# Two-block transformer on one core: the layers' first loads inside the causal projection, and four masked units ahead of each attention loop

## The reference, cut to what matters

```
x = x + causal_attention(layernorm(x)) @ wo + bo        # 16 heads of 16
y = layernorm(x)                                        # then two layers on y:
for l in range(2):
    q, k, v = split(shift_token(y) @ wqkv[l])            # 8 heads of 64
    q, k = rotary_xpos(l2norm(q) * q_scale, l2norm(k) * k_scale)
    y = y + local_attention(q, k, v) @ wo2[l]            # window 128, looks one window back
    y = y + (a * gelu(g)) @ w2[l] + b2[l]                # a, g = split(ln(shift(y)) @ w1[l] + b1[l])
x = x + y
```

## Time and profile before

| | us |
|---|---|
| median of 3 runs (2271.04 to 2278.29) | 2271.34 |
| the profiled execution | 2281.7 |
| its span, first to last instruction | 2280.0 |
| PE busy in it | 1991.5 (87%) |
| DVE, ACT, POOL busy | 1458.2, 1243.6, 798.6 |

### The profile page before, as it was taken

The page is one execution under the profiler, slowest core; times in us unless marked ns, Lnnn a source line. Parts: engine busy times, 40 slices in busy tenths (PEclk is TensorE's granted clock), DMA queues, the critical chain, the costliest instruction groups (busy, mean ns, idle before and its releaser), DMA issues.

```text
span 2280.0 us, 36416 instructions
## 1 busy us (share of the span) xinstructions
PE 1991.5 (87%) x12096; PEld 1254.8 (55%) x12096; DVE 1458.2 (64%) x3958; ACT 1243.6 (55%) x2980; POOL 798.6 (35%) x663
## 2 busy tenths in 40 slices
PE   4565899999989745999999999999899899899998
PEld 2232233333323433677677677677667667667666
DVE  5457788888886334756756755756756756756654
ACT  1110666666666422764764764764664664664663
POOL 2223221221132225614614614614623623623620
PEclk9786899999999877999999999999999999999999
DMA  5645765435631361000000000010300000000000
GB/s 145 148 130 113 132 145 85 69 69 74 121 62 72 107 191 49 40 20 19 1 20 19 1 20 19 2 68 15 103 20 19 20 20 19 20 19 20 20 2 28
DMA packets 124457, 129.00 MB, mean 57 GB/s; under 512 B 50460, under 2 KB 101232, under 8 KB 123248
## 3 DMA queue, kind: packets, MB, share of 16 engines
q1 hardware_dynamic: 123696, 117.75, 22.3%
q0 software_dynamic: 576, 8.91, 1.0%
HBM read 75.51 MB, written 50.86 MB: 55 GB/s over the span
## 4 chain that ended last, share of the span: by engine, by line
PE 37%; DVE 11%; ACT 7%; issue 5%; POOL 2%; DMA 0%; DVEq 0%; SPq 0%; POOLq 0%; ACTq 0%
PE qkv_ps L1340 5%; DVE rot_s L1894 5%; PE s_ps L1444 4%; PE o_ps L1525 3%; PE pt_ps L1525 3%; PE s_ps L1386 3%; PE qkv_ps L1402 3%; PE pt_ps L1457 3%; PE o_ps L1482 3%; DVE p_sb L1903 3%; ACT p_sb L1638 3%; PE pt_ps L1444 2%; PE o_ps L1444 2%; POOL inv_norm L1788 2%; PE s_ps L1402 2%
## 5 line engine op out<-in xcount | busy, mean ns | idle before, releaser
L717 ACT ACTIVATE probs<-st_ps 128x512 f32<-128x512 f32 (+3 forms) x768 | 330.0, 494 | 170.7 <-PE st_ps L625 170.4
L1340 PE MATMUL qkv_ps<-w_qkv,x_parts 128*128 128x512 f32 x1152 | 308.5, 411 | 33.8 <-DVE x_parts L1868 24.6
L1638 ACT ACTIVATE p_sb<-p_sb,negmax 128x256 f32<-128x256 f32 (+1 forms) x512 | 249.2, 489 | 64.3 <-DVE negmax L1903 64.1
L610 PE MATMUL s_ps<-k_stack,q_stack 96*128 96x512 bf16 (+3 forms) x768 | 243.2, 348 | 41.5 <-DVE piece_negmax L762 25.9
L762 DVE CUSTOM_DVE_ANT_0 seen<-s_ps,causal 128x128 f32<-128x128 f32 (+3 forms) x512 | 233.6, 484 | 46.9 <-PE s_ps L610 46.7
L1340 PEld LDWEIGHTS qkv_ps<-w_qkv,x_parts 128*128 128x128 f32 x1152 | 211.9, 194 | 81.5 <-issue 40.0
L625 PE MATMUL st_ps<-q_stack,k_stack 98*128 98x512 bf16 (+3 forms) x768 | 242.3, 336 | 15.7 <-ACT probs L717 10.1
L1903 DVE CUSTOM_DVE_ANT_0 p_sb<-s_ps,band 128x256 f32<-128x256 f32 (+1 forms) x512 | 185.4, 401 | 88.8 <-PE s_ps L1386 85.6
L844 POOL TENSOR_SCALAR_AFFINE_SELECT probs<-probs 128x512 f32<-128x512 f32 x128 | 81.6, 637 | 419.5 <-ACT probs L717 419.5
L1796 POOL TENSOR_TENSOR rot_c<-qn,turn_by 128x512 f32<-128x512 f32 x128 | 178.6, 1415 | 129.6 <-PE turn_ps L1366 103.7
L1654 ACT COPY p_t<-pt_ps 128x512 f32<-128x512 f32 (+1 forms) x256 | 143.2, 559 | 126.0 <-PE pt_ps L1457 124.7
(11 more groups left out here) (146 smaller groups left out, 3504.2 us busy)
## 6 DMA issues: line engine op xcount, KB each, us to landing
qk_scratch<-parts SPq DMA_DIRECT2D x64, 192.0 KB, 2.8
q_stack<-qk_scratch SPq DMA_DIRECT2D x96, 128.0 KB, 6.7
k_stack<-qk_scratch SPq DMA_DIRECT2D x96, 128.0 KB, 7.1
w_ffn<-ffn_weights POOLq DMA_DIRECT2D x4, 2176.0 KB, 11.4
v_scratch<-v_out SPq DMA_DIRECT2D x32, 256.0 KB, 2.5
v_sb<-v_scratch SPq DMA_DIRECT2D x16, 512.0 KB, 10.5
x_in<-xt_scratch SPq DMA_DIRECT2D x16, 512.0 KB, 4.2
ffn_weights<-w_high SPq DMA_DIRECT2D x2, 2176.0 KB, 7.9
```

The costliest lines, as they stand in the source:

```text
L610: pe.matmul(s_ps[i % 3][:, 0:kw], q_stack[0:STK, slot, h, qt * P:(qt + 1) * P], k_stack[0:STK, slot, h, k0:k0 + kw], start=True, stop=True ...
L717: act.activation(probs[:, n % 3, h, q0:CH], st_ps[i % 3][:, q0:CH], ACT.Exp).then_inc(exp_done.sem, 1)
L1340: mm = pe.matmul(qkv_ps[:, part * CH:(part + 1) * CH], x_parts[:, w % XR, xp, k, :], w_qkv[:, wp, k, part * INNER:(part + 1) * INNER], sta ...
L1638: act.activation(p_sb[:, u % 4, h, k0:PW], p_sb[:, u % 4, h, k0:PW], ACT.Exp, scale=-1.0, bias=negmax[:, u % 4, h:h + 1], accum_out=total[ ...
```

## The change

It does three things. First, memory for the projection weights, their raw form, the head scales, the tables and the first x_in is taken before `project_causal`, and `att_in` (now eight tiles) and `x_all` stay allocated to the end; several buffers of `layers` are laid over them. SP loads the first eight tiles of attention output at the end of `causal_attention`, and within `project_causal` it issues the weights at steps 4 and 5, the tables at steps 6 to 9, the scales at steps 10 to 13 and the first sequence at steps 20 and 21; ACT casts the weights and DVE scales the tables during the third sequence, DVE subtracts during the fourth. The transposed half is now stored five tiles behind. `layers` no longer does this for layer 0. Second, `EARLY` is 4: at the end of a feed-forward (and ahead of pass 0) four units are scored and masked, tile 1's turns, the q and k projection of tile 3, and the unit vectors and sines of tile 2 are done there too. Third, in the loop DVE masks two units at once, at even u, ahead of x_parts, sums and unit vectors.

```diff
@@ causal_attention, SP
+            def load_first_outputs():
+                att_tiles, att_in = out_in
+                for c in range(NC):
+                    sp.wait_ge(att_stored[c], 16 * (NG + 1))
+                for t in range(AR):
+                    load_outputs(sp, a, att_tiles, t).then_inc(att_in[t], 16)
...
+            load_first_outputs()
             store(B * NG - 1, 1)
@@ project_causal, SP
+            def load_first(i):
+                half, quarter = HD2 // 2, NT // 4
+                for k in range(KD):
+                    if i == NT // 2 + k:
+                        sp.dma_start(raw_w[:, k, :], a["wqkv"][0, k * P:(k + 1) * P, :]).then_inc(raw_in, 16)
+                for q in range(4):
+                    if i == NT - 2 + q:
...
+                for j, name in ((0, "q_scale"), (2, "k_scale")):
...
+                for k in range(KD):
+                    if i == 2 * NT + NT // 2 + k:
+                        for s in xt_stored:
+                            sp.wait_ge(s, 16 * 2)
+                        sp.dma_start(x_first[:, k, k:k + T], a["xt_scratch"][0, k]).then_inc(x_in, 16)
...
             for i in range(B * NT):
+                load_first(i)
...
-                if i + 4 < B * NT:
-                    load(i + 4)
-                store_xt(i - 3)
+                if i + AR < B * NT:
+                    load(i + AR)
+                store_xt(i - 5)
@@ project_causal, ACT
+                if b == 2 and tile(0) is not None and 0 <= tile(0) < 3 * KD:
+                    high_weights(tile(0))
@@ project_causal, DVE
+                if tile(0) is not None and 0 <= tile(0):
+                    if b == 2:
+                        scale_tables(tile(0))
+                    if b == 3 and tile(0) < 3 * KD:
+                        low_weights(tile(0))
@@ layers
-EARLY = 2
+EARLY = 4
@@ layers, PE, attention
-                    if p < 2 and w + 1 < NT:
+                    if p < 2 and 0 < w < NT - 1:
                         turn(it, w + 1, p)
...
-                    if p >= 1 and w + AHEAD < NT:
+                    if u == 2:
+                        project(it, AHEAD, 2)
+                    if p >= 1 and 0 < w < NT - AHEAD:
                         project(it, w + AHEAD, p - 1)
@@ layers, PE, feed_forward (the same behind scores(0, 0) ahead of pass 0)
                 down(1, 0)
+                if more:
+                    turn(it + 1, 1, 0)
+                    scores(it + 1, 1)
+                    turn(it + 1, 1, 1)
                 down(1, 1)
+                if more:
+                    for part in range(2):
+                        project(it + 1, AHEAD, part)
@@ layers, ACT
+            def first_exponentials(it):
+                for u in range(EARLY):
+                    if u >= 2:
+                        copy_turned(it, 1, u - 2)
+                    exponentials(it, u)
@@ layers, DVE, attention
+                    if EARLY <= u < UNITS and u % 2 == 0:
+                        mask_scores(it, u)
+                        mask_scores(it, u + 1)
                     if p == 2 and w + AHEAD + 1 < NT:
                         low_x(it, w + AHEAD + 1)
                     if p == 3 and w + AHEAD < NT:
                         sums(it, w + AHEAD)
-                    if EARLY <= u < UNITS:
-                        mask_scores(it, u)
@@ layers, DVE, feed_forward
                     mask_scores(it + 1, 0)
+                    mask_scores(it + 1, 1)
                     sums(it + 1, 2)
                 output(1, 0)
                 if more:
-                    mask_scores(it + 1, 1)
+                    mask_scores(it + 1, 2)
+                    mask_scores(it + 1, 3)
+                    unit_vectors(it + 1, 2)
+                    times_sin(it + 1, 2)
                 output(1, 1)
```

More of the change, by code:

```diff
@@ L865, in project_causal @@
         w_o = sb("w_o", [P, KD, D])
-        att = sb("att_in", [P, 4, NG, GF])
+        att, att_in = out_in
+        w_qkv, raw_w, head_scale, turn_by, x_first = first
         att_t = sb("att_t", [P, 2, KD, P])
@@ L1584, in _ @@
             scores(0, 0)
+            turn(0, 1, 0)
+            scores(0, 1)
+            turn(0, 1, 1)
+            for part in range(2):
+                project(0, AHEAD, part)
             for it in range(LAST):
```

160 lines of the change are left out of this document (93 added, 67 removed).

## The result

| | before | after |
|---|---|---|
| median | 2271.2 (4 runs, 2268.9 to 2278.3) | 2242.7 (4 runs, 2236.1 to 2247.1) |
| profiled execution, span | 2281.7, 2280.0 | 2243.9, 2242.1 |

The ratio is 0.9867, with an interval of 0.983 to 0.990: 28.5 us faster, where 45 were forecast. The range of the prediction (2208 to 2247) holds the time, and its sign was right; 16.5 us of the gain are missing. The two profiled executions differ by more, 37.9 us, because that of before is a long one: its causal projection begins (SP issues the load of w_o) at 762.94, that of after at 756.23. In the 14 profiles of this study this point lies between 751.7 and 762.9.

The account below looks back on a forecast made before the run. TensorE was busy 87%, its waits being load latency at the layers' start, att_in in the projection and DVE's masking in the loop. Terms -19.0 - 8 - 8.2 + 2.4 - 12 = -45 took the 2271.3 median to 2226, range 2208 to 2247.

Parts of the forecast that it names:

- Start of the layers: Before the layers' first projection matmul: loads, casts and table products moved away, 19.0 us less, ends 18.5 and 19.2.
- Rival (e): Start of the layers: a moved load lands late, half of the 19 is lost; 2236, chance 0.05.
- Causal projection: Stage before the layers: deeper att_in buffering removes queue stalls, 8 us gained; ends 12.4 gained and 6 lost.
- rival (b): Projection stage becomes bound by DMA, x1 stores and scales queuing behind loads: +6 in place of -8; 2240, chance 0.13.
- DVE's additions lie mostly in its idle half: Causal projection: eight table products (0.41 each) and six subtractions (at most 0.9) fit mostly where DVE idles.
- Windows of the loop: Attention loop: paired masking removes TensorE's 0.52 us wait in windows 2 and 3; 8.2 us less over eight passes.
- Boundary and window 1: Between passes: 2.06 us masking wait gained, 0.5 given back in window 1; net 1.5 each, 12 less.
- Last windows: End of each pass: layer norm's normalising stands behind one more masking, +0.3 each, +2.4 over eight.
- the forecast's -17.8 over eight: Attention loop, first scores to last scores: windows, last windows and boundary together, -8.2 + 2.4 - 12.
- Rival (a): Attention loop does not pay, the freed wait reappears behind ACT: -25, 2246, chance 0.16.
- (c): Whole kernel: everything waited for goes, -19 - 12.4 - 30.0 = -61; 2210, chance 0.08.
- (d): Loop slower: vectors end over 4.33 us after scores, TensorE follows; output delays transposes; +20, 2291, chance 0.04.

Follow-up runs that it names:

- order_only: Kernel before with only the loop's new orders (EARLY 4, paired masking, moved turns), loads as before: 2266.1 us, ratio 0.9962.
- loads_only: Changed kernel with early loads and deeper att_in, but the loop's order of before: 2252.2 us, ratio 0.9906.
- single_late: Changed kernel with units 26 to 31 masked one by one again: 2238.4 us, ratio 0.9849.
- ffn_later: Changed kernel with POOL issuing the second layer's feed-forward weights behind tile 2's rotation in pass 4: 2241.3 us in one run.
- sums_first: Changed kernel with VectorE's sums of tile 3 ahead of the low part of tile 4's x in window 0: 2233.6 us in one run.

## Why the prediction was right or wrong

**Start of the layers: right.** 19.0 forecast, 18.84 measured, by the mechanism given: the last affine select, one subtraction of 0.41 (0.76 for the two that overlap), and signalling, of which there is 0.27 in place of 0.1. Rival (e) falls.

**Causal projection: the mechanism was half right, the size was not.** Forecast 8.0; measured 4.8 in the pair, and 4.6 if the mean of eight executions (70.75) is set against the two that have the old stage (76.65 and 74.09 in `order_only`). The waits for att_in did go. The step of the sum that was mis-sized is the choice of "8 us of gain, nearer to TensorE's end because the queue's stalls are what the deeper buffer removes": the stalls were not removed but moved from TensorE's loads to VectorE's stores and scales (9.1 and 3.4 us), and TensorE stands 8.6 us behind VectorE in place of 2.3. It is the place that rival (b) named, but its price was too high: the stage never came near 77. The Trainium skill (DMA: Bandwidth & Descriptors, section "Queues, rings and completion order") says that an engine works through a queue's descriptors in order; the k scale, issued behind weights and tables and waited for 3.4 us, agrees. "DVE's additions lie mostly in its idle half" held to within 2 us: DVE was busy 6.00 of 6.00 us from 810 to 816, yet the kernel without them has a stage of 68.87.

**Windows of the loop: right in sum, in part by luck.** Unit vectors 12.32 us apart, 12.43 forecast. By the clean passes 5 and 6 of after against those of `loads_only`, windows 2 to 4 are 0.2, 0.6 and 0.2 us shorter, 1.0 in all; 1.04 was forecast, as 0.52 for windows 2 and 3 and nothing for 4. In window 3 the vectors end 4.13 us behind the scores and the projection starts at 4.33, as forecast. In window 2 they still carry the lateness of window 1: they wait for POOL's inverse norms, end at 4.54, and the projection starts at 4.69, 0.36 late, in all eight passes.

**Boundary and window 1: larger in clean passes than forecast, but not all passes are clean.** Window 0 with the boundary gives 2.2 and window 1 0.1 in the second layer's clean passes (2.65 and -0.45 in the first layer's): 2.2 to 2.3 where 1.5 was forecast. The forecast's own terms for the unit vectors of tile 3 give 1.1 us late (1088.4 + 1.22 against 1084.2 + 4.33), not the 1.3 that it puts down; 1.41 was measured. And the rows that it took for this window, are of pass 1, one of the two in which the kernel before has the low clock: the granted clock is 0.54 from 1086.6 to 1090, and the 13.23 is 12.87 in six of the eight passes.

**Last windows: mis-sized.** +0.3 was forecast ("behind one more masking"); measured +1.1 to +1.4 a pass. Two more maskings stand on the layer norm's chain, as `single_late` showed. It is the place where the sum erred most: TensorE stands 10.5 us for `hn` in place of 0.2.

The errors of boundary and last windows nearly cancel: a clean pass is 2.2 us shorter than one of `loads_only` (170.7 against 172.85), and the forecast's -17.8 over eight is -2.2 each. That these agree is luck.

Beside this, from first scores to last scores, 11 us of the forecast are missing:

- 2.9 us: the loads make each way from one pass to the next longer by 0.4, a cost for which the prediction has no term. Shown by `loads_only`; the cause is open.
- 3.4 us: window 1 of pass 4 (16.75 in place of 13.3). The step that failed is that a moved operation was not followed past POOL's queue: the load of w_ffn waits there for the last down projection, and the rotation of tile 2, whose inputs now come earlier, stands behind it. Shown by `ffn_later`.
- 3.2 us: the clock in window 1 of passes 0 and 1 (15.0 and 14.8 in place of 13.3). The prediction saw the unit vectors of tile 3 come 1.3 us late, and 1.41 was measured; it did not ask what TensorE's standing would do to its clock. That the clock is the price is shown by the windows at 0.50; that a shorter wait does not remove it, by `sums_first`. The kernel before had such dips too, at 0.36 us each; what the change added is mostly that they fall on TensorE's path.
- 1.5 us: what is left of the two errors over eight passes, boundary and window 1 (-17.5 without the two items above, where -12 was forecast) and last windows (+9.4, where +2.4 was). Windows 2 to 4 have -8.2, as forecast.

Rival (a), "the loop does not pay", came nearest in time (2246), but by none of its own mechanism: no new wait behind ACT appeared, and the loop's orders alone gave 8 us. Rivals (c) and (d) fall by the time. But what (d) describes is there in small: its threshold (vectors over 4.33 us behind the scores) is crossed in window 2 of every pass (4.54) and in window 1 (5.0 to 5.7, in pass 4 7.5), and from there TensorE follows the vectors. That is the growth of its wait for them from 8.6 to 18.7 us. The chances as stated, with the 0.02 for no change, add up to 1.02.

## What to carry to other kernels

When work is moved ahead, write down for every engine's list, GpSimd's DMA issues too, which waiting instruction the moved work now stands behind, and how many instructions are now ahead of each short chain (here a layer norm), instead of pricing the one that is in view. When a new wait of 1 to 2 us lands on TensorE, look at the granted clock behind it in each pass: here it doubled the price. A DMA-heavy stage that stalls by name on one buffer may stall on the next one when that is deepened; take the price of the stage, not that of the wait.

## What the hardware showed that was not expected

**The clock falls in fixed passes.** Nearly the same waits (0.76 and 1.4 to 1.5 us) are followed by clock 0.50 in passes 0 and 1 and by 1.00 in 2 and 3, twice in the same way, and one edit in the causal projection, 50 us and more before the first of them, changed which. In `single_late`, which is as fast or faster elsewhere, six of eight passes have it, among them pass 6, whose waits (0.76 and 0.88) are those that the changed kernel has there at full clock; some 5 of 9.5 us go back. What decides in which pass the clock falls stays open. So a single run of such a kernel can hide or double a small gain, and two runs of it repeat the same error.

**A subtraction of 0.41 us took 1.52 and 2.38.** In windows 2 and later of the changed kernel, VectorE's subtraction of x_parts (both inputs in SBUF) meets POOL's rotation. Pass 3 of after:

```profile
1404.63 2.39 POOL L1883 TENSOR_TENSOR x_all<-x_all,rot_s 128x1024 f32<-128x1024 f32 x1 [0.76 <-DVE rot_s L1976]
1405.79 1.52 DVE L1950 TENSOR_TENSOR x_parts<-x_in,x_parts 128x256 fp32r<-128x256 f32 x1
```

It ends 0.29 us after POOL's instruction does (1407.31 and 1407.02), whenever it was issued; in pass 4 it was issued 0.26 behind POOL's and took 2.38. The Trainium skill (SBUF — State Buffer, section "SBUF: two separate sides") says that a VectorE operation with two SBUF inputs and a GpSimd operation that reads SBUF exclude each other for a whole instruction, and this agrees. It adds some 25 us of busy VectorE to the kernel. In windows 3 and 4 it costs nothing: the unit vectors at 1083.70 and 1096.02 start right behind the maskings, not behind the norms. In pass 4 it was on the path.

**The causal projection scatters by 4 us from one execution to the next** (69.4 to 73.4 with the same code), and where it begins by 11. An edit there of less than that can't be judged by one profile.
